# All keys and values of a four-layer model made inside the first layer's scan

## The reference, cut to what matters

```python
# layer 1: Mamba; 16 states n, a scan over the 512 positions
def step(state, inp):
    d, b, c, u = inp
    dA = jnp.exp(d[..., None] * A)
    state = state * dA + (d * u)[..., None] * b[:, None, :]
    y = jnp.einsum('bdn,bn->bd', state, c)
    return (state, y)
...
y = y + D[None, :, None] * x
y = y * silu(z)                      # z is the layernorm of the residual stream
...
# layer 4: attention; k and v depend on the context alone
k = (encoder_hidden_states @ Wk).reshape(B, Skv, H, D)      # H = 16 heads of 128
v = (encoder_hidden_states @ Wv).reshape(B, Skv, H, D)
```

## Time and profile before

| | |
|---|---|
| median of 3 runs | 3708.42 us (3700.74 to 3710.17) |
| profiled execution | 3708.7 us, its span 3707.1 us |
| busy: TensorE, VectorE, ScalarE, POOL | 3437.8, 3013.5, 1759.9, 623.9 us |
| stage 0 | up to about 727 us |
| stage 4 | about 2012 to 2086 us |
| mean granted clock of TensorE | 0.966 |

### The profile page before, as it was taken

How to read it: one execution, slowest core, us unless ns; L and a number is a source line. 1 busy time by engine, 2 the same in 40 slices (tenths; PEclk the granted TensorE clock), 3 DMA queues, 4 the chain that set the end, 5 groups by cost and what they waited for, 6 DMA issues and landing times.

```text
span 3707.1 us, 40267 instructions
## 1 busy us (share of the span) xinstructions
PE 3437.8 (93%) x12305; PEld 1947.9 (53%) x12322; DVE 3013.5 (81%) x4951; ACT 1759.9 (47%) x2748; POOL 623.9 (17%) x596
## 2 busy tenths in 40 slices
PE   7888888799999999899999899999999999999887
PEld 4667676544444444444445788655455455455443
DVE  8899998797979798789889867688388388388797
ACT  6878787633333223334443311255155155155297
POOL 2324251243433220134331000000000000000000
PEclk9899988999999999999999999999999999999998
DMA  4324241524342322443444300221021022021000
GB/s 156 133 65 148 66 147 59 196 86 147 102 153 93 137 84 92 156 153 97 149 156 175 145 24 23 104 70 60 31 70 60 21 70 70 20 70 64 32 12 34
DMA packets 91260, 345.73 MB, mean 93 GB/s; under 512 B 11841, under 2 KB 20161, under 8 KB 77793
## 3 DMA queue, kind: packets, MB, share of 16 engines
q1 hardware_dynamic: 61552, 226.90, 17.4%
q0 software_dynamic: 29552, 116.94, 9.6%
HBM read 280.88 MB, written 62.91 MB: 93 GB/s over the span
## 4 chain that ended last, share of the span: by engine, by line
PE 48%; DVE 27%; issue 14%; ACT 6%; DMA 3%; DVEq 0%; POOL 0%; ACTq 0%; POOLq 0%; SPq 0%
PE ps L1213 30%; PE ps L1610 6%; PE ps L1600 3%; DVE room L1782 3%; PE ps L1441 2%; DVE room L1786 2%; DMA room<-bc_scratch 2%; DVE room L1790 2%; PE ps L1493 2%; PE ps L1282 2%; DVE room L1852 1%; DVE room L1795 1%; DVE room L1850 1%; ACT room L871 1%; DVE room L2320 1%
## 5 line engine op out<-in xcount | busy, mean ns | idle before, releaser
L1213 PE MATMUL ps<-lnT,room 128*128 128x512 f32 x2240 | 987.0, 596 | 23.1 <-DVE room L2007 16.0
L1213 PEld LDWEIGHTS ps<-lnT,room 128*128 128x128 f32 x2240 | 426.0, 191 | 567.9 <-issue 525.5
L1213 PE MATMUL ps<-room 128*128 128x512 f32 (+2 forms) x1807 | 666.8, 524 | 49.6 <-ACT room L1138 21.1
L680 POOL TENSOR_TENSOR idle<-idle 128x1 f32<-128x1 f32 x268 | 447.1, 1668 | 1263.4 <-ACT room L881 434.6
L1213 PEld LDWEIGHTS ps<-room 128*128 128x128 f32 (+1 forms) x1824 | 289.9, 163 | 404.5 <-issue 258.4
L1441 PE MATMUL ps<-room 128*128 128x512 f32 x864 | 379.7, 597 | 8.5 <-DVE room L1961 8.5
L792 ACT ACTIVATE room<-room,small 128x511 f32<-128x511 f32 x256 | 163.6, 710 | 380.6 <-DVE room L1786 380.5
L1852 DVE TENSOR_TENSOR_SCAN room<-room 128x2048 f32<-128x2048 f32 x64 | 283.2, 4425 | 19.0 <-ACT room L871 13.8
L1786 DVE TENSOR_TENSOR_SCAN room<-room 128x2048 f32<-128x2048 f32 x64 | 283.4, 4428 | 5.9 <-DVE room L1782 0.9
L1441 PEld LDWEIGHTS ps<-room 128*128 128x128 f32 x864 | 165.1, 192 | 215.2 <-issue 208.3
L1112 ACT ACTIVATE room<-ps,stat 128x512 f32<-128x512 f32 x256 | 199.0, 777 | 137.3 <-DVE stat L2268 137.3
(11 more groups left out here) (284 smaller groups left out, 5105.1 us busy)
## 6 DMA issues: line engine op xcount, KB each, us to landing
room<-in_ffn SPq DMA_DIRECT2D x16, 2048.0 KB, 10.9
room<-bc_scratch POOLq DMA_DIRECT2D x128, 256.0 KB, 3.6
room<-kv_stash SPq DMA_DIRECT2D x64, 512.0 KB, 3.4
kv_stash<-room POOLq DMA_DIRECT2D x96, 256.0 KB, 2.4
room<-stash POOLq DMA_DIRECT2D x24, 1024.0 KB, 5.2
room<-in_ffn SPq DMA_DIRECT2D x20, 1024.0 KB, 5.1
room<-in_ffn SPq DMA_DIRECT2D x24, 768.0 KB, 5.6
room<-in_ffn SPq DMA_DIRECT2D x12, 1536.0 KB, 7.3
```

Of the source, the lines that this page charges most:

```text
L680: nc.gpsimd.tensor_tensor(idle[:, :], idle[:, :], idle[:, :], ALU.add).then_inc(zeros_added, 1)
L1213: last = nc.tensor.matmul(out, lhsT, rhs, start=(i == 0), stop=(i == len(parts) - 1))
```

## The change

- `KV_ORDER` has 16 slots instead of 12, and all 16 heads of each batch are made in stage 0: 12 own ones, in states 1 to 11, and the first 4 of the next batch in states 12 to 15. In states 6, 8, 9 and 10 stand two.
- The load of the next batch's context into `m_kctx` is behind the row of state 15 instead of 10.
- The store of m_z is behind row 9 (and the store of the next batch's B and C rows) instead of row 8.
- The units of `gate_mamba`, their loads, copies and stores, their semaphores and the waits of later stages on them go away. `widen(0, 2)` and `widen(2, 4)` are joined ahead of gate 3.

```diff
-KV_HEADS, KV_LEAD = 12, 4
-KV_OWN = KV_HEADS - KV_LEAD
-KV_ORDER = (4, 5, 6, 6, 7, 8, 8, 9, 10, 11, 12, 13)
+H, KV_LEAD = 16, 4
+KV_OWN = H - KV_LEAD
+KV_ORDER = (1, 5, 6, 6, 7, 8, 8, 9, 9, 10, 10, 11, 12, 13, 14, 15)
...
-                        if n == 10 and not last:
+                        if n == 15 and not last:
                             sp.wait_ge(tile_filled, tile("kv", KV_OWN - 1, 1)[0] + 1)
                             sp.dma_start(m_kctx, ctx_d[bass.ds(b * P + P, P), :]).then_inc(kctx_loaded, 16)
...
                         if n == 9 and not last:
                             store_bc(0, b + 1, tile("x", 0)[0])
-                        if n == 8:
+                        if n == 9:
+
                             place = stashed(2, b)
                             sp.wait_ge(Du_ready, b + 1)
                             sp.dma_start(place, m_z).then_inc(Du_stored, 16)
...
-                units(0, 1)
                 gate(0)
-                units(1, 2)
                 gate(1)
-                units(2, 5)
                 gate(2)
-                widen(0, 2)
-                units(5, 9)
-                widen(2, 4)
+                widen(0, 4)
                 gate(3)
                 widen(4, 6)
-                units(9, 13)
                 take_lnT(stage + 1, 0)
                 widen(6, EARLY)
-                units(13, B * LATE)
...
-                pe.wait_ge(gkw_loaded, LATE * 16)
-                units(0, 3)
                 gate(0)
-                units(3, 6)
                 gate(1)
-                units(6, 10)
                 gate(2)
-                units(10, 13)
-                pe.wait_ge(gk_taken, 26)
                 transpose_ln(stage + 1, 0)
                 gate(3)
                 pe.wait_ge(lnT_ready, B * LNT[stage + 1] + 1)
-                units(13, B * LATE)
```

More of the change, by code:

```diff
@@ L631, in attention3 @@
                 for parity in range(2):
-                    sp.wait_ge(kv_stored[parity], B * KV_HEADS * 16)
-                for i in range(3):
-                    sp.wait_ge(gk_stored[i], GK_STORES[i] * 16)
+                    sp.wait_ge(kv_stored[parity], B * H * 16)
                 for h in range(2):
@@ L702, in store_kv @@
                                b * KV_WAITS + (KV_FIRST + 2 * i),
-                               None if last and i + 2 >= slots else (h + 2) % KV_HEADS, i)
-            def store_late(k):
-                b, h = k // LATE, KV_HEADS + k % LATE
-                wait(gk_taken, 2 * k + 2, KV_ALL + 2 * (B * (4 + 2 * STATES) - 2) + k)
-                pool.dma_start(kv_stashed(b, h), g_kv[k % 3]).then_inc(gk_stored[k % 3], 16)
+                               None if last and i + 2 >= slots else (h + 2) % H, i)
             def feed_states(stage, s):
@@ L910, in body @@
                         if early is not None:
[L911 removed]
+                            take_kv(early, b * (H * 16) + (KV_LEAD + early) * 16, tile)
                         if n == 2:
@@ L923, in body @@
                         if late is not None:
-                            take_kv(late, b * (KV_HEADS * 16) + (KV_LEAD + late) * 16, tile)
+                            take_kv(late, b * (H * 16) + (KV_LEAD + late) * 16, tile)
                         if n == 6:
@@ L980, in gate @@
                     nc.scalar.activation(g_z[b % 2], ln[:, :], ACT.Silu).then_inc(g_z_ready, 1)
-                def units(first, last):
-                    for k in range(first, last):
-                        if k >= 3:
-                            act.wait_ge(gk_stored[k % 3], k // 3 * 16)
-                        for half in range(2):
-                            act.wait_ge(gk_filled, 2 * k + half + 1)
-                            nc.scalar.activation(g_kv[k % 3][:, half * 4 * HD:(half + 1) * 4 * HD],
-                                                 ps[:, 4 + 2 * (k % 2) + half, :], ACT.Copy).then_inc(gk_taken, 1)
                 def widen(first, last):
@@ L1358, in gate_mamba @@
             def gate_mamba(stage):
-                w4 = g_kvw.rearrange("p (i c n) -> p i c n", i=LATE, c=CK)
-                def units(first, last):
-                    for k in range(first, last):
-                        b, i = divmod(k, LATE)
-                        if i == 0:
-                            pe.wait_ge(gk_loaded[b % 2], b // 2 * 16 + 16)
-                        if k >= 2:
-                            pe.wait_ge(gk_taken, 2 * k - 2)
-                        for half in range(2):
-                            for j in range(2):
-                                t = 2 * half + j
-                                mm = product(ps[:, 4 + 2 * (k % 2) + half, j * 256:(j + 1) * 256],
-                                             [(g_kctx[b % 2][:, c, t * P:(t + 1) * P], w4[:, i, c, :]) for c in range(CK)])
-                            mm.then_inc(gk_filled, 1)
                 def gate(b):
@@ L2066, in body @@
                             t = g * n + j
-                            if first and t == n:
-                                for i in range(3):
-                                    dve.wait_ge(gk_stored[i], GK_STORES[i] * 16)
                             dve.wait_ge(up_done, b * T + (base + t + 1))
```

41 lines of the change are left out of this document (8 added, 33 removed).

## The result

The changed kernel takes 3759.7 us (median of 4 runs, 3753.38 to 3763.61) against 3709.3 us for the one before (4 runs, 3700.74 to 3714.5). The ratio on record is 1.0129, 95% interval 1.0107 to 1.0151; the medians alone would give 1.0136. The profiled execution took 3759.13 us, its span 3757.5 us against 3707.1 us. So its trace is 50.4 us longer than that of before, and that is the sum to be explained. The forecast had the sign and most of the places, and about half of the size: 28.5 us.

What follows compares the result with a forecast made beforehand. VectorE leads narrowly (157.9 of 170.6 us a batch), but its waits decide. Three full batches at 7.5 + 2, plus 3 for the last, minus 3 for the gate stage: +28.5 us on 3708.7, 3737; range 3707 to 3758.

Steps and rivals of the forecast that it cites:

- the 3751 that the forecast gave itself: Upper end of the forecast's own case, 3718 to 3751 us, inside the wider range of 3707 to 3758.
- Full batches of 179 to 181 us: First layer: a sign that the forecast is right, the length of batches that also prepare a next one.
- Row 9: Before state 9: VectorE's wait of 4.41 us for the row of B goes, 18.4 us in the layer.
- Slot 0 in state 1: State 5: the moved unit delays ScalarE's decay behind x_proj and costs VectorE about 2.5 us.
- Two units in states 9 and 10: ScalarE ends exp_abs at 515.5 behind the second unit of state 9; VectorE reaches the next softplus 5.2 us later than before.
- State 13: Scan of state 13 late by 5.2, 9.5 or 12.4 us; 7.5 taken per full batch, replacing the 5.2.
- y: States 14 and 15: two more units on TensorE delay VectorE's multiplication of y up to 3.1 us; 2 taken.
- Last batch: States 9 and 10 hold two units each there too: scan of state 13 is 0 to 5 us late; 3 taken.
- Gate stage: Units leave: 9.4 us back, less 6.4 for a lower clock; 3.0 us gained, bounds 0 and 9.4.
- the stores bound: Rival, chance 0.15: ScalarE waits for its own store at every second unit, TensorE's addition is late; +51.5 us, 3760.
- hidden: Rival, chance 0.10: units fit into idle time of TensorE and ScalarE, and row 9 gives its 18.4 us; 3681.
- the forecast's request that waits out a scan: State 10: the second half's store request waits out state 11's scan, putting scan 13 at 544.3, 12.4 us late.

## Why the forecast was right in sign and too small

*Against the range.* The median of 3759.7 us lies 1.7 us above the upper end of 3758; the ratio on record puts it at 3757 (1.0129 × 3709.3). So it is at the edge of the range, and above the 3751 that the forecast gave itself. Full batches of 179 to 181 us were named as a sign; the second and third took 186.8 and 184.7.

*Row 9.* Right: the waits of 4.4 to 4.7 us for bc_scratch are gone, and in the trace no row waits in their place. Right also that the gain would not stay: alone in the kernel before, 18.4 us of waits were worth about 8, by the trace of the first layer 2.7.

*Slot 0 in state 1.* The size and the state were right (2.5 forecast, 2.23 measured, in state 5), the path was not: the multiplication waits for TensorE's transposes, while the scan waits its 2.72 us for the decay as before.

*Two units in states 9 and 10, ahead of exp_abs.* The mechanism was right. The forecast had the softplus wait "about 10 us" for L846; it waits 8.3 to 8.5. It had 5.2 us net of the row's gain; in the changed kernel 2.23 − 4.41 + 6.44 is 4.3, and with four half-buffers and the weights' own queue the whole batch is 5.4 longer.

*State 13.* Taken as 7.5 us late (bounds 5.2, 9.5, 12.4); by the rows above 4.3 + 2.25, so 6.5. But the step said that this is the end of it, since VectorE then "has no waits to give back" and TensorE only keeps up. In states 12 to 15 the copies still wait for stores, so VectorE stood 2.0 to 3.3 us at the addition L1758 ahead of state 15 (0.2 before). This wait has no term in the sum. With it a full batch, y apart, was 9.5 (with the 0.6 from ahead of it), 11.7 and 10.0 us longer: 31.2 against 22.5.

*y.* Forecast 2 us, at most 3.1; measured 3.98, 4.15 and 4.15, 12.3 in three. The bound held only if the units start when TensorE is free. With four half-buffers it is 1.73 and 3.47 in the second and third batch, with the weights' own queue too 0.55 at most.

*Last batch.* This is the step that failed most: "0 to 5 us late; I take 3". Without the y of the batch before it, it was 12.5 us longer (softplus −4.0, row −4.6, against 21.7 us of waits in states 12 to 14, less 0.5 that before had there). The forecast took the steps of a full batch over, where a bad case costs 12.4 once. It did not follow the loop from copy over POOL and landing back to the copy, nor the weights that stand behind the stores in the same queue. The runs put a number on both: four half-buffers shorten this batch from 191.1 to 185.5 us, the weights' own queue to 175.6. Spreading the units out gives 2.0 us back by the trace.

*Gate stage.* Forecast −3.0 (0 to −9.4); measured −2.4 in the change, −3.3 with the units left out of the kernel before. The terms were too large on both sides and nearly cancel: the four waits for transposes fall from 8.0 to 6.0 us (5.0 back forecast), three of the four groups of additions take 3.31 instead of 2.73 us, 1.7 in all (4.4 forecast), and the wait for the first product falls from 8.45 to 6.51 us (4.5 less 2 forecast). The forecast's 1.1 us a gate comes to 1.16 by its own numbers (0.44 + 3 × 0.24), and 5.0 + 4.5 to 9.5; neither changes the forecast by more than 0.3 us. The 0.92 us that the forecast has for four transposes is a quarter of the 3.68 in the earlier trace rows, measured after 6.46 us idle, and its half clock is the 0.50 in the earlier trace rows. The trace of the kernel after has both: four times in this stage 16 transposes took 3.65 to 3.68 us, each time after 8.0 to 19.6 us idle, and a fifth group directly behind one of them 2.14; the granted clock was 0.50 from 2110 to 2125 and 0.57 in the whole stage, with TensorE busy 16.6 of 68.7 us. The first result of the fp8 layer came 6.4 us after the layer's start (2136.06 to 2142.46), 2.4 more than before, where the forecast took 2; the clock was 0.50 from 2135 to 2140, 0.86 in the next 5 us and 1.00 in the 5 after. What makes it fall is not shown.

*Sum.* Forecast 3 × 9.5 + 3 − 3 = 28.5. Measured 31.2 + 12.3 + 12.5 = 56.0 in the first layer, −2.4 in the gate stage and −3.2 in the stages around it, 50.4. The time fell on the rival "the stores bound", 3760, but by its mechanism in part only, so that the number met it is luck: its price of 12.4 us at state 13 never came (6.5), and the stores took their share in state 15, at y and in the last batch instead. Of the 50 us the runs put about 30 on the half-buffers, some 10 on the weights in the last batch (by the trace). What is left, 11 us by the medians and 16.8 by the profiled spans (3723.9 against 3707.1), is 16.1 us in three batches, the units' work and order, and 1.2 in the last, less 0.5 outside the first layer. The "hidden" rival fell because totals of free time (21 us of TensorE) say nothing of who stands in front of exp_abs.

*POOL's small instruction.* The small instruction ahead of a store took 3.87 and 3.94 us beside scans of the last batch, and 0.18 us where it was shortest. At the place shown above it ends with the scan that ran beside it (713.15 and 713.17):

```profile
708.74 4.43 DVE L1779 TENSOR_TENSOR_SCAN room<-room 128x2048 f32<-128x2048 f32 x1
```

This is no single case. Of the 121 such instructions between 90 and 790 us, 73 took over 0.5 us, and every one of the 73 ends within 0.06 us of the end of a VectorE instruction; a moment picked at random does so in 7 of 100 cases. Of the 44 that took 0.25 us or less only five ran wholly inside a VectorE instruction, and that was the multiplication of y, which reads PSUM. In the kernel before it was 66 of 98, again all 66 within 0.06 us; the 3.59 us in the earlier trace rows end at 497.16, the scan beside them at 497.17. So where the small instruction is long, it ends when VectorE's instruction does, and the forecast's request that waits out a scan is what these traces show. Why the two end together is not shown: no experiment put another instruction in its place. That the way over POOL is what delays the stores is (15.1 instead of 81.8 us of waits with the stores on ScalarE's queue).

What stays open: why the stages outside the first layer and the gate stage were 3.2 us shorter in this trace (the four runs of the kernel before spread over 13.8 us), and how much of the last 11 us could go with an order that has fewer units before state 13.

## What to carry to other kernels

Work moved into the idle time of busy engines is paid by the queue and the buffers it shares, not by the engines' totals: follow one unit round its whole loop (compute, copy, issue, landing, buffer free) at the new rate before counting any idle time, and do so for the last iteration too. A removed wait is worth only what the next engine in line is early by; here 18.4 us of waits gave 8 us, and 18 together with doubled half-buffers. And before moving work out of a stage, take it out there and look at the stage: 58 us of TensorE were worth 3.

## What the runs showed of the hardware

- POOL's instruction on a single column took 0.18 to 3.96 us in 118 times of the first layer of the kernel after (90 to 770 us; median 1.15, mean 1.3), and whenever it took over 0.5 us it ended within 0.06 us of the end of a VectorE instruction.
- A store of 256 KB landed at a median of 2.6 us (2.4 before); beside a 1 MB store and row loads, 700 to 720 us, 3.9 was the median of six, and beside the first loads of the feed-forward (run with the last batch spread out) one took 8.6 us.
- The granted clock of the gate stage was 0.57 with the units gone (0.95 before), with 80 matmuls of TensorE in it, 16.6 of 68.7 us, and 16 transposes after 10 us of idling took 3.68 us (1.91 where TensorE had not paused):

The gate stage of the kernel after, TensorE in order of time:

```profile
2112.05 3.68 PE L1317 MATMUL ps<-ident,room 128*128 128x128 f32 x16 [10.23 <-DVE room L1864]
```
